# A hybrid block on one core: what the second weighing waits for, and attention stages written out slot by slot

## The reference

```python
x = x + attn_a(layernorm(x))   # 16 heads of 64: a normalised running state, then causal softmax attention
x = x + ffn(layernorm(x))      # mixture of 16 experts, 8 of them chosen, and a shared one
x = x + attn_b(layernorm(x))   # a transformer of 6 layers with linear attention, 16 heads of 8
x = x + ffn(layernorm(x))
```

```python
Qp, Kp = favor_phi(q), favor_phi(k)                    # exp(u - nrm), exp(-u - nrm), 16 features a head
scores = where(tril, Qp @ Kp.T, 0)                     # in chunks
num = scores @ V + Qp @ (sum of Kp.T @ V before)
out = num / (den + 1e-6)
h1 = layer_norm(x + out @ Wo + bo)
x = layer_norm(h1 + relu(h1 @ W1 + bf1) @ W2 + bf2)
```

## Time and profile before

| | |
|---|---|
| median of 3 runs | 3992.89 us (3991.1 to 4001.3) |
| profiled execution | 4006.08 us, span 4004.3 us |
| mean granted TensorE clock | 0.957 |
| TensorE busy | 3529.4 us, 88% of the span |
| VectorE, ScalarE, GpSimd busy | 2578.8, 1705.0, 901.3 us |
| attention stage / first experts | about 105 to 1585 us / 1585 to 2010 us |
| transformer stage / second experts | about 2010 to 3630 us / 3630 to 4004 us |

### The profile page before, as it was taken

How to read it: one execution, slowest core, us unless ns; L and a number is a source line. 1 busy time by engine, 2 the same in 40 slices (tenths; PEclk the granted TensorE clock), 3 DMA queues, 4 the chain that set the end, 5 groups by cost and what they waited for, 6 DMA issues and landing times. The chain is left out here.

```text
span 4004.3 us, 104912 instructions
## 1 busy us (share of the span) xinstructions
PE 3529.4 (88%) x39640; PEld 2752.3 (69%) x39640; DVE 2578.8 (64%) x6838; ACT 1705.0 (43%) x3438; POOL 901.3 (23%) x781
## 2 busy tenths in 40 slices
PE   4999999999999998899578988888888888886998
PEld 3767676767677776788456666666666666665887
DVE  4555555555565555787766666666766667666887
ACT  2555555555555555333233333333333333322332
POOL 3222232223232232000012222222222222221000
PEclk9999999999999999999799999999999999997999
DMA  2000000000000000000000000000000000000000
GB/s 86 26 27 24 26 24 26 22 27 24 28 22 26 24 23 18 1 1 0 13 15 2 2 16 2 16 2 2 16 2 2 16 2 2 2 2 1 1 0 21
DMA packets 38329, 59.48 MB, mean 15 GB/s; under 512 B 6960, under 2 KB 16688, under 8 KB 37552
## 3 DMA queue, kind: packets, MB, share of 16 engines
q1 hardware_dynamic: 37936, 53.78, 4.0%
HBM read 18.10 MB, written 2.10 MB: 5 GB/s over the span
## 5 line engine op out<-in xcount | busy, mean ns | idle before, releaser
L662 ACT ACTIVATE a_prob<-a_s,a_shift,a_scale 128x128 f32<-128x128 f32 (+3 forms) x512 | 312.0, 613 | 485.4 <-DVE a_shift L745 485.3
L1194 ACT COPY t_num<-t_n 128x512 f32<-128x512 f32 x96 | 56.3, 586 | 649.7 <-PE t_n L1005 649.7
L1542 ACT ACTIVATE ffn_silu<-ffn_ps_g 128x512 f32<-128x512 f32 x272 | 161.3, 599 | 381.9 <-PE ffn_ps_g L1492 369.8
L944 POOL TENSOR_TENSOR t_rstd<-t_var_eps,minus_half 128x4 f32<-128x4 f32 x96 | 97.6, 1017 | 1002.7 <-DVE t_var_eps L1256 1002.7
L1485 PEld LDWEIGHTS ffn_ps_y<-moe_down,ffn_hidden 128*128 128x128 f32 x2176 | 282.1, 191 | 40.0 <-issue 18.5
L1005 PE MATMUL t_n<-t_mixed,t_v_pad 128*32 128x64 f32 x6144 | 199.4, 230 | 123.1 <-ACT t_phi_q L1190 95.2
L1485 PE MATMUL ffn_ps_y<-moe_down,ffn_hidden 128*128 128x128 f32 x2176 | 288.1, 275 | 15.9 <-DVE ffn_acc L1646 15.9
L1005 PEld LDWEIGHTS t_n<-t_mixed,t_v_pad 128*32 128x32 f32 x6144 | 163.3, 116 | 171.1 <-issue 171.1
L1646 DVE SCALAR_TENSOR_TENSOR ffn_acc<-ffn_ps_y,ffn_combine,ffn_acc 128x128 f32<-128x128 f32 x960 | 269.7, 345 | 9.0 <-DVE ffn_acc L1646 1.9
L742 DVE TENSOR_REDUCE a_neg_max<-a_s 128x2 f32<-128x256 f32 (+3 forms) x256 | 208.8, 816 | 72.5 <-PE a_s L565 70.0
L1658 DVE TENSOR_TENSOR ffn_hidden<-ffn_silu,ffn_ps_u 128x512 f32<-128x512 f32 x272 | 185.5, 684 | 105.2 <-ACT ffn_silu L1542 74.5
(11 more groups left out here) (209 smaller groups left out, 8837.3 us busy)
## 6 DMA issues: line engine op xcount, KB each, us to landing
a_k_swap<-a_k_own SPq DMA_DIRECT2D x128, 128.0 KB, 2.1
a_y_swap<-a_y_own SPq DMA_DIRECT2D x128, 128.0 KB, 2.0
a_staged<-in_pairs SPq DMA_DIRECT2D x8, 384.0 KB, 3.3
t_next<-in_t_w SPq DMA_DIRECT2D x12, 256.0 KB, 3.0
t_next_rows<-in_t_rows SPq DMA_DIRECT2D x6, 448.0 KB, 4.4
x<-in_x SPq DMA_DIRECT2D x8, 256.0 KB, 5.4
out<-x SPq DMA_DIRECT2D x1, 2048.0 KB, 8.7
t_next_sq<-in_t_sq SPq DMA_DIRECT2D x6, 256.0 KB, 2.6
```

Of the source, the lines that this page charges most:

```text
L662: nc.scalar.activation(prob[c % 2][h][:, 0:(c + 1) * P], ps[f"s{h}"][:, 0:(c + 1) * P], ACT.Exp, bias=shift[:, k:k + 1], scale=scale[slot. ...
```

## The change

Two edits. In `pipeline`, which both attention stages use, the inner loop goes: slots 1 to 5 of each layer are written out like the others, and only the loop over layers stays. In `attend`, the second weighing (A1, t = 1) waits for s0 to s3 up to the first step of its slot, so for the fills of the slot before, and no longer for those of its own slot's mapq. A0 waits as before, as its own position is named outright.

```diff
-UNROLLED = 2
...
-        with e.Fori(0, (B - 4) // UNROLLED) as tn:
-            for u in range(UNROLLED):
-                z = tn * UNROLLED + (1 + u)
-                run(slot(z, (1 + u) % 2), {"in": z + 1, "next": z + 2, "out": z - 1})
-        run(slot(B - 3, 1), {"in": B - 2, "next": B - 1, "out": B - 4})
+        for z in range(1, B - 2):
+            run(slot(z, z % 2), {"in": z + 1, "next": z + 2, "out": z - 1})
         run(slot(B - 2, 0, build=None if final else l + 1), {"in": B - 1, "next": B, "out": B - 3})
...
                     wait_free(pe, bank, slot, f"A{t}")
                     for r in range(4):
-                        wait_free(pe, f"s{r}", slot, f"A{t}")
+                        wait_free(pe, f"s{r}", slot, "A0" if t == 0 else slot.steps[0])
                     pe.nop(nofuse=True)
```

## The result

The changed kernel takes 3833.4 us (median of 4, 3828.6 to 3837.8) against 3995.4 us for the kernel before on the same chip (median of 4, 3991.1 to 4001.3). The ratio is 0.959, with a 95% interval of 0.9576 to 0.9604: 162 us less. Forecast were 3842 us and a range of 3800 to 3905.

What follows compares the result with a forecast made beforehand. TensorE was taken as the bound, busy 3529.4 of 4004.3 us. Transformer-stage and lead savings of 149.3 us, with 2 for the attention stage, gave 151 off: 3855 profiled, 3842 median, range 3800 to 3905.

Steps and rivals of the forecast that it cites:

- The wait before A1: Transformer stage: A1's 2.07 us wait for phi_q goes in each slot, so a plain slot falls from 30.7 to 28.6 us.
- The inner jumps: Transformer stage: six TensorE jumps go; a slot behind one takes 4.4 us over plain.
- The outer jump: Transformer stage: the jump between layers stays; of its 6.5 us over plain, 5.0 are left.
- Straight code's stops: Transformer stage: written-out slots pay for instruction fetching, 0.8 us a slot in the five looped layers, 1.6 in the last.
- The term of 1.6: Last transformer layer: fetching costs 1.6 us in each of five slots, as that layer already shows such stops.
- The premise behind these terms: Transformer stage: slots 1 to 4 ran from instructions already there; written out they pay like slots 5 to 8, mean 2.4 us.
- The attention stage: Attention stage: writing out its inner loop gains 0; at most 3 us cost for the loop's ends, 2 taken.
- straight code is paid in full: Rival: each written-out transformer slot pays 2.4 us, A1's gap or not; 83 us off, 3910 us; chance 0.17.
- the wait moves: Rival: h1, keys or A1's copy end up 2 us late, giving back 95.2 us; 3937 us; chance 0.05.
- it isn't gone: Rival: another count reached by phi_q holds A1 and fetching eats the loops' gain; within 0.3%; chance 0.03.
- the kernel gets slower: Rival: fetching falls behind in every slot, costing over 4.0 us in all eight; at 5.0 some 4035 us; chance 0.02.
- fetching hides entirely: Rival: written-out slots pay nothing for fetching; 191 us off, 3802 us; chance 0.13.

Runs made afterwards that it cites:

- wait_only: Kernel before with only A1's wait changed, both inner loops kept: 3853.2 us, ratio 0.9649 to the kernel before.
- pad121 kernels: Changed kernel with 121 idle semaphore instructions ahead of TensorE's transformer-stage work, once with A1's old wait (3998.5 us), once with the new (3860.0 us).
- pad121_old_wait: Changed kernel with A1's old wait and 121 idle semaphore instructions ahead of TensorE's transformer-stage work: 3998.5 us, ratio 1.0011 to the kernel before.
- attention_loop_kept: Changed kernel, but the attention stage keeps its inner loop: 3831.5 us, ratio 0.9595 to the kernel before.
- pad141_new_wait: Changed kernel with 141 idle semaphore instructions ahead of TensorE's transformer-stage work: 3836.7 us, ratio 0.9603 to the kernel before.
- pad101_new_wait: Changed kernel with 101 idle semaphore instructions ahead of TensorE's transformer-stage work: 3839.8 us, ratio 0.9601 to the kernel before.
- loops_only: Changed kernel with A1's old wait, so only the inner loops written out: 3954.6 us, ratio 0.9895 to the kernel before.

## Why the prediction was right

- **The wait before A1** was right in mechanism and size. The 95.2 us are gone, h1, mapk and ScalarE's copy wait for nothing new, and a plain slot without a stop takes 28.5 in wait_only (forecast 28.6). This is shown by wait_only, where only the wait was changed.
- **What depends on it** was under-weighed. I counted the stops inside A1 as a cost of straight code that partly stays, and left out those at mapk. With the wait gone, 18 us of 23 go at once (wait_only), and the pair of pad121 kernels shows that without the wait the same places make only short ones.
- **The inner jumps** were right: 6 waits at the turn fewer, 20.3 us, and with clock 4.4 us each as in the earlier trace rows (33.2 against 28.9 in wait_only: 4.3).
- **The outer jump** was right: 4.6 over a slot of 28.5, forecast 5.0. The fifth layer's last slot has 1.5 over instead of 2.9.
- **Straight code's stops** moved to the scores, as forecast (11.0 us in 24, none over 1.0 us); at A0, where I expected more too, there is one of 0.3 us in the last slot. Their size was forecast at 0.8 a slot in looped layers and 1.6 in the last; the slots not behind a jump average 29.15, so 0.65 over 28.5, and the last five (145.2 - 5 x 28.5) / 5 = 0.5. The 0.65 is more than the listed stops, but it lies in the same place: even in a slot without a listed stop S1 takes longer than in a slot of 28.5 us. First slot 4 of the fourth layer (29.0 us), then a slot of wait_only (28.5):

```profile
2843.80 2.46 PE L977 MATMUL t_s<-t_phi_q,t_kz 32*128 32x64 f32 x64
```

```profile
2970.24 2.01 PE L981 MATMUL t_s<-t_phi_q,t_kz 32*128 32x64 f32 x64
```

  The term of 1.6 is the one that was mis-sized most. With the code where it was and only the wait gone, the last layer still pays about that: four of its slots take 29.5 to 30.5 in wait_only, 1.0 to 2.0 over 28.5. In the changed kernel the ends have moved, and three of its five slots have no stop (28.4 to 28.6).
- **The premise behind these terms** was wrong. Nothing shows slots 1 to 4 running "from instructions already there": behind the jump into slot 3 the turn waited 3.01 us, and taking this loop away cost no packet (303 before, 295 with the attention stage's loop kept). They were free of stops by their place: by the count below the ends lay 172 and 191 instructions into A1 in them, and with the old wait no stop came with less than 198. That written-out slots pay less than 2.4 thus came true partly by luck of where the new code lies; pad121_old_wait, with the same code 121 instructions further, took 3998.5 and not 3954.6.
- **The sum.** A looped layer came to 948.7 / 4 = 237.2 against 240.2 (0.8 from plain slots, 0.4 from the outer jump, 1.8 from stops), times 4 is 12.0; the fifth 2.9 less, the last five slots 5.8 less, the lead and the attention stage 7.0 off instead of 4.1. Together 23.6 on top of 151, so 174.7 between the two profiled spans. Between the medians it is 162, as the profiled execution before was 10.7 us above its median in this comparison and the one after 2.0 below. So 3833 and not 3842: 9 us, a fifth of a percent. The nearness is in part luck. Between profiled executions 151 was forecast, and it was 174.7. The prediction took the profiled execution after to lie above its median by the same 13 us as the one before; it lies 2 below.
- **The attention stage** gained nothing in itself, as taken (attention_loop_kept). The first F2 of the transformer stage comes 7.0 us earlier than before, of which A1's one wait in the lead is 2.1. 4.2 of the 7.0 lie ahead of the stage's first turn (1992.4 before, 1988.2 after); wait_only, whose attention stage is unchanged, has 1989.1, so most of these come from no edit.
- **The rivals.** That straight code is paid in full (3910) fails at the stops of 0.65 instead of 2.4. That the wait moves, that it isn't gone, and that the kernel gets slower fall with the list of waits. That fetching hides entirely (3802) came nearer than its 0.13: what it would still save is the 0.5 to 0.65 us a slot, some 27 us. Against it stand the 24 stops of up to 1.0 us at L977 in the changed kernel's trace.

## What to carry to other kernels

A wait whose releaser belongs to the same slot, while the data come from an earlier one, can cost more than its own length. Here 95 us of waits were worth 143: without them TensorE was busy for 40.9 us less with the same instructions, and its stops in A1 and at mapk fell from 23.4 us to 5.6. So price a wait with what comes right after. A jump back in an unrolled pipeline can have a price of its own (here mostly 4 to 5 us of TensorE for bodies of 960 to 3,840 matmuls and as many weight loads, up to 9 in one placing, and nothing to be seen for one of 392), and writing out only pays where that price is seen: the inner loop of the attention stage was free to keep, its outer one was not. In the straight code here the stops behind the remaining waits cost 0.5 to 0.65 us a slot; shifting them with padding moved that cost but earned nothing.

## What the runs showed of the hardware

**Where the stops lie.** I numbered TensorE's instructions in the compiled order and looked up the one ahead of which each stop of the transformer stage not behind a jump stands. This is my own count, not a view of the profile:

```
before   10252 11275 12300 14861 15886 16911 17935 18191   modulo 256: 11 to 15
after    10481 11506 13554 15602 16625 21491 22515 23539   modulo 256: 241 to 243
```

In each kernel these stops fall on one place modulo 256, within a few instructions, and other kernels with other shifts showed the same (241 to 245 with 53 to 180 padding instructions, 5 to 7 in attention_loop_kept). In this stage only the 3.5 us ahead of the last slot's first transposes (L1095) do not: they are the same in every kernel, wherever they lie, and what they wait for is open. The few short stops at L561 (L557 after) in the attention stage, at most 0.6 us, stand at other places. The queue's packets are 16 KB each (303 in 4.96 MB). From these two, the 16 KB and the step of 256, my estimate is that instructions come 256 at a time here, 64 bytes each. Whether such an end was felt went with what was ahead of it: with the old wait the stops in A1 and at mapk came when it lay 198 to 242 instructions into A1 (0.2 to 2.2 us, most above 1), and with the new wait they are at most 0.6 us in the same places.

**A jump back** in the transformer stage stopped the turn for 2.9 to 3.7 us in most kernels and for 3.5 to 4.3 in the pad121 kernels, pad141_new_wait, attention_loop_kept and pad101_new_wait; a second stop of 2.3 to 2.8 us came in the pad121 kernels alone, whose jump lands 5 instructions ahead of an end. With 25 (pad101), 125 (after) and 241 (pad141) instructions ahead of the next end there was none. Why the first stop is longer in some kernels no run here shows. By the same count the body of the transformer stage's inner loop is 2015 instructions long and the turn behind its jump waits (3.0 to 3.1 us in five layers of the kernel before and 3.5 in the last), while that of the attention stage is 882 long and its slots take 23.2 us inside and outside the loop.

**The padding has a price.** With 121 to 180 idle instructions ahead of the stage, the stage's first turn waits 43 to 52 us for "issue" where it waited some 39 us for ScalarE's o_now otherwise; at 101 it still waits for o_now (39.7 us). Each further one adds 0.15 us, and 180 put the stage's first F2 back by 15 us.

**VectorE** is busier by 57 us for the same 6838 instructions. In the four looped layers 41 us of it lie in one group, the four t_kz of a slot (128x512), whose mean rose from 495 to 829 ns while the idle time ahead of it fell from 135.5 to 26.4 us. This goes with the wait's edit: VectorE is busy for 2629.5 us in wait_only and 2577.5 in loops_only. What makes the records longer was not tried; no wait of TensorE's in the changed kernel is put down to t_kz.
